# Working a mixture of experts with the weights stationary: Silu straight from PSUM, no turning of the hidden rows, three sets of weight buffers, sixteen groups written out

## What is computed

```python
def _swiglu(x, g, v, o):
    return jax.nn.silu(x @ g) * (x @ v) @ o
scores = jax.nn.softmax(x @ w_router.T, axis=-1)          # 64 experts
topw, topi = jax.lax.top_k(scores, 6)
combine = zeros.at[arange(T)[:, None], topi].add(topw)
routed = sum over 64 experts of combine[:, e] * _swiglu(x, wg[e], wv[e], wo[e])
shared = _swiglu(x, swg, swv, swo)                        # every token
return routed + shared                                     # then layernorm(x + ...)
```

## Time and profile before

| | us |
|---|---|
| median of three runs | 992.77 |
| lowest, highest | 991.32, 993.33 |
| span of the profiled execution, first to last instruction | 985.7 |
| median less span | 7.07 |
| groups of the experts, first weights matmul to last | 521.27 to 698.7 |

### The profile page before, as it was taken

The page is one execution under the profiler, slowest core; times in us unless marked ns, Lnnn a source line. Parts: engine busy times, 40 slices in busy tenths (PEclk is TensorE's granted clock), DMA queues, the critical chain, the costliest instruction groups (busy, mean ns, idle before and its releaser), DMA issues.

```text
span 985.7 us, 15418 instructions
## 1 busy us (share of the span) xinstructions
PE 870.2 (88%) x5267; PEld 568.3 (58%) x5271; DVE 720.6 (73%) x1377; ACT 510.4 (52%) x1022; POOL 407.1 (41%) x338
## 2 busy tenths in 40 slices
PE   7999999999999999988889999999546867899886
PEld 3466666666565666656666777677423654343443
DVE  5667786959696867768774556665467798998797
ACT  3563554545544444445444334455522457898485
POOL 0203448494848577534214333333377312221013
PEclk9999999999999999989999999999866998999998
DMA  5451212112131221100926999999633000000001
GB/s 189 153 196 27 65 49 86 70 65 77 58 102 53 81 75 65 44 1 1 238 94 216 298 311 310 313 312 303 179 96 98 26 1 3 5 8 6 1 6 38
DMA packets 54743, 106.46 MB, mean 108 GB/s; under 512 B 8909, under 2 KB 26645, under 8 KB 54165
## 3 DMA queue, kind: packets, MB, share of 16 engines
q1 hardware_dynamic: 48917, 89.88, 29.6%
q0 software_dynamic: 5760, 15.74, 6.0%
HBM read 88.45 MB, written 17.14 MB: 107 GB/s over the span
## 4 chain that ended last, share of the span: by engine, by line
PE 54%; DVE 19%; DMA 10%; issue 5%; ACT 5%; SPq 3%; POOL 3%; DVEq 0%; ACTq 0%; POOLq 0%
PE ps L777 10%; PE ps L715 6%; DMA w_dn<-in_w_dn 5%; PE ps L873 5%; PE ps L725 4%; DVE row_max L2696 3%; PE ps L948 3%; DMA y_dram<-y_out 3%; PE ps L1280 3%; POOL key_part L1507 2%; DVE state L2119 2%; PE ps L795 2%; PE ps L960 2%; DMA key_part<-y_dram,slot_idx 2%; PE ps L1266 2%
## 5 line engine op out<-in xcount | busy, mean ns | idle before, releaser
L1479 POOL DMA_INDIRECT xg<-x_dram,tok_of x68 | 65.1, 958 | 131.8 <-PE ps L1006 94.2
L777 PE MATMUL ps<-w_vg,xT 128*128 128x512 f32 x256 | 116.8, 597 | 1.2 <-DVE th L2162 1.2
L1429 POOL TENSOR_TENSOR state<-state,rows_bc 128x1024 f32<-128x1024 f32 x22 | 53.8, 2446 | 95.5 <-DVE state L2119 41.9
L715 PE MATMUL ps<-xT,w_qks 128*128 128x512 f32 x192 | 86.5, 596 | 5.2 <-ACT qT L1585 5.2
L948 PE MATMUL ps<-w_gv,xgT 128*128 128x352 f32 (+1 forms) x272 | 87.4, 464 | 2.5 <-DMA w_dn<-in_w_dn 2.4
L2696 DVE TENSOR_REDUCE row_max<-ps 128x4 f32<-128x1024 f32 x64 | 74.3, 1217 | 7.1 <-PE ps L1245 6.3
L2130 DVE TENSOR_TENSOR aT<-ps,tri 128x768 f32<-128x768 f32 x64 | 59.7, 954 | 27.0 <-PE ps L725 26.9
L1585 ACT ACTIVATE probT<-ps 128x512 f32<-128x512 f32 x128 | 69.5, 594 | 10.1 <-PE ps L1266 9.6
L777 PEld LDWEIGHTS ps<-w_vg,xT 128*128 128x128 f32 x256 | 45.8, 190 | 48.8 <-issue 43.1
L960 PE MATMUL ps<-w_dn,hidT 88*128 88x256 f32 (+1 forms) x272 | 70.0, 379 | 0.0
L948 PEld LDWEIGHTS ps<-w_gv,xgT 128*128 128x128 f32 x272 | 48.9, 190 | 27.0 <-issue 5.2
(11 more groups left out here) (327 smaller groups left out, 2066.6 us busy)
## 6 DMA issues: line engine op xcount, KB each, us to landing
w_gv<-in_w_gv SPq DMA_DIRECT2D x68, 352.0 KB, 8.2
rows_bc<-x_dbl_dram SPq DMA_DIRECT2D x32, 512.0 KB, 3.8
w_dn<-in_w_dn SPq DMA_DIRECT2D x68, 192.0 KB, 9.6
y_dram<-y_out SPq DMA_DIRECT2D x68, 128.0 KB, 7.5
y_dram<-blank SPq DMA_DIRECT2D x4, 1408.0 KB, 13.2
w_vg<-in_wvg SPq DMA_DIRECT2D x8, 512.0 KB, 4.9
w_qks<-in_wqks SPq DMA_DIRECT2D x8, 384.0 KB, 3.1
w_o<-in_wo SPq DMA_DIRECT2D x8, 256.0 KB, 2.7
```

Of the source, the lines that this page charges most:

```text
L715: last = mm(bank(PJ + n % 2), w_qks[:, k, part * P:(part + 1) * P], xT[:, k, half * 512:(half + 1) * 512], start=(k == 0), stop=(k == KD - 1))
L777: last = mm(bank(PJ + t % 2), xT[:, k, t * P:(t + 1) * P], w_vg[:, k, :], start=(k == 0), stop=(k == KD - 1))
L1429: G.tensor_tensor(state_of(m), state_of(m), c_row[:, n % 2], ALU.mult).then_inc(read_out, 1)
L1479: G.indirect_dma_start(xg[:, j, :], None, x_dram, bass.IndirectOffsetOnAxis(ap=col, axis=0)).then_inc(gathered[j], 16)
```

## The change

The up projection is turned: the weights are stationary and the activations `xgT` (128 columns) move, so that the hidden values come out with the hidden index on the partitions, as the down projection wants them. The 176 hidden columns are cut in 112 and 64 (`FA`, `FB`). "gate" and "value" of the first 112 go to one PSUM bank for a pair of blocks; "low" has the last 64 of the gate and of the value in one 128-column weight, so that its gate stands on partitions 0 to 63 and its value on 64 to 127. ACT takes Silu directly; DVE multiplies once. `turn_hid`, `hidT_of` and the tanh form are gone, as are the factors 0.5. Down is one matmul of 112 rows for a block and one of 64; the 64-row matmuls of a pair of blocks lie on different rows of the array and write different banks. The work is signalled by pairs of blocks, and the results of a whole group are signalled together: `down_ready` once a group, two copies of 512 columns on DVE, two stores of 256 KB with rows of 2 KB (`y_rows`, `y_pair`), which puts slots in another order, which `slot_idx` takes into account with four more small DVE instructions.

Weights are three DMAs a block: `w_up` 352 KB (rows of 2816 bytes as before), `w_dn` 112 rows of 1 KB, `w_low` 64 rows of 1 KB. `RING` is 3, all twelve blocks are asked for ahead without waits between. For group i SP stores a pair and asks for that pair of group i + 3. Stores 14 and 15 are issued by ACT. The overflow groups all use one set. On PE and SP the sixteen groups are written out. The shared expert is worked the same way, four tiles (512 columns) at once.

```diff
-FH = F // 2
-FP = 96
+HIGH = 64
+FA, FB = F - HIGH, HIGH
+UP = 2 * F
-RING = 2
+RING = 3
+LAST_SET = FIXED % RING
+def y_rows(i, p):
+    rows = y_dram[bass.ds(i * (NJ * P) + p * 2 * P, 2 * P), :]
+    return rows.rearrange("(r two) d -> r (two d)", two=2)
...
-            for dst, src in ((sh_gv, "sh_gv"), (sh_dn, "sh_dn"), (pos, "pos"), (ident_bf, "ident_bf"),
+            for dst, src in ((sh_up, "sh_up"), (sh_dn, "sh_dn"), (sh_low, "sh_low"), (pos, "pos"), (ident_bf, "ident_bf"),
...
             for r in range(RING):
                 for j in range(NJ):
-                    if r:
-                        sp.wait_ge(w_loaded[j], 32 * r)
-                    load_block(r * NJ + j, j, w_gv[:, r * NJ + j], w_dn[:, r * NJ + j])
+                    load_block(r * NJ + j, j, r)
...
-            with sp.Fori(0, FIXED // RING - 1) as d:
-                for r in range(RING):
-                    for j in range(NJ):
-                        store_y(d * RING + r, j)
-                        sp.wait_ge(w_loaded[j], at(d, 32 * RING, 32 * (r + RING)))
-                        sp.sem_inc(load_due, 1)
-                        load_block(d * (RING * NJ) + ((r + RING) * NJ + j), j, w_gv[:, r * NJ + j], w_dn[:, r * NJ + j])
+            for i in range(FIXED - RING):
+                for p in range(2):
+                    store_y(i, p)
+                    sp.wait_ge(w_loaded[i % RING][p], LOADS * (i // RING + 1))
+                    for j in (2 * p, 2 * p + 1):
+                        load_block((i + RING) * NJ + j, j, i % RING)
...
+            def group(i, r, uses):      # PE
...
                 for p in range(2):
+                    pe.wait_ge(xgT_copied, at(i, 2, p + 1))
+                    pe.wait_ge(hid_ready, at(i, 4, HIDDEN - 4 + p + 1))
+                    for o in range(2):
+                        j = 2 * p + o
+                        if o == 0:
+                            pe.wait_ge(w_loaded[r][p], uses * LOADS)
+                        up(ps[0:FA, p, 2 * o * P:(2 * o + 1) * P], w_of(j), "gate", x_of(j))
+                        last = up(ps[0:FA, p, (2 * o + 1) * P:(2 * o + 2) * P], w_of(j), "value", x_of(j))
+                    last.then_inc(up_ready, 1)
+                for p in range(2):
+                    pe.wait_ge(hid_ready, at(i, 4, HIDDEN - 4 + 2 + p + 1))
+                    for o in range(2):
+                        last = up(ps[:, 2 + p, o * P:(o + 1) * P], w_of(2 * p + o), "low", x_of(2 * p + o))
+                    last.then_inc(up_ready, 1)
+                pe.wait_ge(down_copied, at(i, 2, COPIED))
+                for p in range(2):
+                    pe.wait_ge(hid_ready, at(i, 4, HIDDEN + p + 1))
+                    for o in range(2):
+                        mm(ps[:, 4 + o, p * D:(p + 1) * D], hidT_a[:, 2 * p + o, :], w_dn[:, r * NJ + 2 * p + o, :],
+                           start=(p == 0), stop=False, skip_group_check=True)
+                    for o in range(2):
+                        turn_g(i + 1, 2 * p + o)
+                for p in range(2):
+                    pe.wait_ge(hid_ready, at(i, 4, HIDDEN + 2 + p + 1))
+                    for o in range(2):
+                        rows = slice(HIGH * o, HIGH * o + FB)
+                        last = mm(ps[:, 4 + o, p * D:(p + 1) * D], hidT_b[rows, p, :], w_low[rows, r * (NJ // 2) + p, :],
+                                  start=False, stop=True, skip_group_check=True)
+                last.then_inc(down_ready, 1)
...
-            with pe.Fori(0, FIXED // RING) as d:
-                for r in range(RING):
-                    group(d * RING + r, lambda j, k: w_gv[:, r * NJ + j, k, :], lambda j, f: w_dn[0:FH, r * NJ + j, f, :])
+            for i in range(FIXED):
+                group(i, i % RING, i // RING + 1)
...
-            def group(i, side=None):    # ACT
+            def group(i, side=None, stored=None):
                 for p in range(2):
+                    act.wait_ge(up_ready, at(i, 4, HIDDEN + p + 1))
+                    f(silu_a[:, 2 * p:2 * p + 2, :], ps[0:FA, p, :].rearrange("p (e two n) -> p e two n", e=2, two=2)[:, :, 0, :],
+                      ACT.Silu).then_inc(silu_ready, 1)
...
             def group(i, first=False, side=None):       # DVE
-                for j in range(NJ):
-                    hidden(i * NJ + (j + TILES), j, 2 * j + 1)
...
+                dve.wait_ge(down_ready, at(i, 1, 3))
+                if not first:
+                    for p in range(2):
+                        dve.wait_ge(y_stored[p], at(i, 16, 0))
+                for o in range(2):
+                    V.tensor_copy(y_out[:, o::2, :], bank(4 + o).rearrange("p (a d) -> p a d", a=2)).then_inc(down_copied, 1)
+                for p in range(2, 4):
+                    if side:
+                        side(p)
```

More of the change, by code:

```diff
@@ L41 @@
 FIXED = E // NJ
-RING = 2
+RING = 3
+LAST_SET = FIXED % RING
+LAST_USES = len(range(LAST_SET, FIXED, RING))
 FAR = 16384.0
@@ L476, in build @@
         gathered = [sem(f"gathered{j}") for j in range(NJ)]
-        w_loaded = [sem(f"w_loaded{j}") for j in range(NJ)]
-        y_stored = [sem(f"y_stored{j}") for j in range(NJ)]
+        w_loaded = [[sem(f"w_loaded{r}_{p}") for p in range(NJ // 2)] for r in range(RING)]
+        y_stored = [sem(f"y_stored{p}") for p in range(NJ // 2)]
         wkv_loaded = sem("wkv_loaded")
@@ L943, in _, with part_of, up @@
             last.then_inc(route_mm, 1)
-            def gate_up(j, x_of, w):
+            def part_of(w, k, part):
+                first = k * UP + dict(gate=0, value=FA, low=2 * FA)[part]
+                return w[:, first:first + (2 * FB if part == "low" else FA)]
+            def up(out, w, part, x_of):
                 for k in range(KD):
[L948 to L960, removed]
-                last.then_inc(down_ready, 1)
[L963 to L977, removed]
+                    last = mm(out, part_of(w, k, part), x_of(k), start=(k == 0), stop=(k == KD - 1))
+                return last
+            Y_SH = (3, 2)
+            def shared_up(h):
+                def x_of(k):
+                    return xT[:, k, h * 512:(h + 1) * 512]
+                if h:
+                    pe.wait_ge(hid_ready, 2)
+                up(ps[0:FA, 0, :], sh_up, "gate", x_of)
+                up(ps[0:FA, 1, :], sh_up, "value", x_of).then_inc(up_ready, 1)
+                if h:
+                    pe.wait_ge(down_copied, 2)
+                up(bank(2), sh_up, "low", x_of).then_inc(up_ready, 1)
@@ L1005, in turn_g @@
                 for k in range(KD):
-                    last = nc.tensor.transpose(ps[:, 2 * j, k * P:(k + 1) * P], xg[:, j, k * P:(k + 1) * P], ident[:])
+                    last = nc.tensor.transpose(ps[:, 6 + j // 2, (j % 2) * D + k * P:(j % 2) * D + (k + 1) * P],
+                                               xg[:, j, k * P:(k + 1) * P], ident[:])
                 last.then_inc(xg_turned, 1)
[L1009 to L1027, removed]
@@ L1498, in _ @@
                     gather(j, tok_cur[:, j:j + 1])
-            for j in range(NJ):
-                pool.wait_ge(y_stored[j], at(used, 16, 0))
+            for p in range(NJ // 2):
+                pool.wait_ge(y_stored[p], at(used, 16, 0))
             pool.sem_inc(gather_due, 1)
@@ new lines, in _, with xgT_of @@
+            silu_shared(0)
+            scale_probs()
+            keep_shared(0)
+            scale_hot(0)
+            silu_shared(1)
+            for t in range(1, TILES):
+                scale_hot(t)
+            act.wait_ge(angle, 8)
+            f(cos_sin[:], ang[:], ACT.Sin).then_inc(cos_sin_ready, 1)
+            act.wait_ge(route_mm, 3)
+            f(expert_row[:], ps[0:1, Y, 0:P], ACT.Copy).then_inc(route_act, 1)
+            keep_shared(1)
+            def xgT_of(i, p, first=False):
+                act.wait_ge(xg_turned, at(i, NJ, 2 * p + 2))
+                if not first:
+                    act.wait_ge(up_ready, at(i, 4, HIDDEN - 4 + 2 + p + 1))
+                f(xgT[:, 2 * p:2 * p + 2, :].rearrange("p a b -> p (a b)"), bank(6 + p), ACT.Copy).then_inc(xgT_copied, 1)
@@ new lines, in store_late @@
+            def store_late(i):
+                act.wait_ge(down_copied, at(i, 2, COPIED + 2))
+                for p in range(2):
+                    act.dma_start(y_rows(i, p), y_pair(p)).then_inc(y_stored[p], 16)
+            def group(i, side=None, stored=None):
+                for p in range(2):
+                    act.wait_ge(up_ready, at(i, 4, HIDDEN + p + 1))
[3 more added lines that the diff above has]
+                        side(p)
+                for p in range(2):
+                    act.wait_ge(up_ready, at(i, 4, HIDDEN + 2 + p + 1))
+                    f(silu_b[HIGH:P, 2 * p:2 * p + 2, :].rearrange("p a b -> p (a b)"),
+                      ps[0:FB, 2 + p, 0:2 * P], ACT.Silu).then_inc(silu_ready, 1)
+                if stored is not None:
+                    store_late(stored)
+                for p in range(2):
+                    xgT_of(i + 1, p)
```

(11 more changed lines are left out.)

237 lines of the change are left out of this document (127 added, 110 removed).

## The result

| | before | after |
|---|---|---|
| median, 20 runs of each, side by side | 987.92 us | 993.96 us |
| ratio of the two, 95% interval | | 1.0067 [1.0045, 1.009] |
| profiled execution, span | 985.7 us | 993.1 us |
| first gather behind the groups (POOL `key_part`) | 703.93 us | 708.65 us |

The changed kernel is 0.7% **slower**, about 6 us, where 9 us faster was forecast. The forecast set out from 992.77, the median of three runs that lay within 0.2% of each other; twenty runs of the kernel before spread from 979.89 to 993.33, with the median at 987.92. Ratios are therefore the fair measure: forecast 983.8/992.77 = 0.991, measured 1.0067.

A forecast was written before the change was run, and what follows sets the result against it. DMA bandwidth was taken to bound the groups, PE 5% behind. Groups ending 10.3 us earlier, 1.3 given back, made net -9.0: span 976.7 plus 7.07 gave 983.8 us; its own range 977 to 990, with rivals 971 to 992.

The forecast's parts named there:

- rival (c): Groups: stores of y set the pace, landing 8.0 + copies 1.36 + issue 0.7 stretching to 10.44 us; 993 us, chance 10%.
- wrong: List of contrary signs: rate under 300, 9.2 us groups throughout, DMA share under 1 during `y_stored` waits, first `tok_of` after 512.3.
- the sum: Groups: loads from 532.0, 46.0 MB at 309 GB/s until 680.9, then 7.5 us of PE, ending 688.4 instead of 698.7.
- The third set: Weights before the groups: 2.16 MB move into the idle stretch; loads starting later give back 4 of its 7 us.
- The DMA's rate: Groups' full stretch: 309 GB/s, the deciding term; 260 GB/s if reads limit gives 981.6 us, 300 and 320 give 988 and 979.
- PE's group: PE per group: 9.24 us (9.0 to 9.8) instead of 9.96, up 5.4, off the path while DMA needs more.
- the 64-row passes: Down projection: two 256-column pairs side by side on the array take 1.22 us a group, 1.74 if not.
- rival (d): Down projection: 64-row pairs don't run side by side, group 9.76 us, still under 10.39; no time change, no separate chance.
- The start of the groups: After routing: moves by 0 to -1.2 us, taken as -0.6, to 520.7.
- The idle stretch: DMA before the groups, 495 to 512 us, nearly idle (0.06) before: filled to about 500 by the added weight loads.
- From PE's end to the first gather: Behind the groups: 1.3 us more, from DVE copies of 1.36 instead of 0.43 and one more store issue of 0.36.
- Rival (b): Groups: PE is the bound if DMA runs above 350 GB/s; 17 x 9.24 = 157 us, time 973, chance 12%.

The follow-up runs named there:

- the one without its other waits: Changed kernel with second set of `y_out`, empty slots' rows spread, `w_up` loads released after the up passes: two weight sets 1.0033, three 0.9874 to the kernel before.
- The kernel with both causes removed: Changed kernel with a second set of `y_out` and the gathered rows of empty slots spread: 979.08 us, 0.9914 to the kernel before.
- the best version: Changed kernel, three weight sets, with second `y_out`, empty slots' rows spread and `w_up` released when the up passes are done: 974.88 us, 0.9874 to the kernel before.
- the first two runs with two sets: Changed kernel with two weight sets instead of three: 1024.52 us, 1.0362; the same with `w_up` released early, stores ahead of small loads: 992.27 us, 1.0053.
- the kernel before and its variant: The variant is the kernel before with the gathered rows of empty slots spread: 988.7 us, 1.0024 to the kernel before.

## Why the prediction was wrong, point by point

**The failed step is the sentence against rival (c)**: "a store is late only because loads stand ahead of it, and then the DMA is working". It left out the time that SP needs to issue. In the changed order six issues of 0.43 to 0.6 us stand on SP between a group's copies and its second store; while they pass, the DMA is not kept full (0.94 and 0.96 up to 600 us), because SP had waited for those copies before it issued any of that group's loads. The rival's sum had 0.7 us of issue where 3.7 passed, and 8.0 of landing where 5.5 were needed. The two errors nearly cancelled (10.06 against 10.5 measured): that the rival's period came out right was luck, and the argument that set it at 10% was wrong. Its sign stood in the text under "wrong": share under 1 while DVE waits for `y_stored`.

PE ended the groups at 703.15 us, 14.8 later than the 688.4 of the sum. An estimate from the forecast's own terms (first group 9.24, last group 9.24, so 9.95 a step between) divides this: 7.7 us in the fourteen steps that the store loop paces (10.50 each), 4.2 in the step to the overflow group (14.1), 1.3 in the last group at the low clock, and 1.6 before the second group's up pass, as the first group took 11.17 us at a granted clock of 0.83 (521.3 to 531.3 us; 1.00 before).

**The overflow's gathers** were in no term. The sum let PE do 7.5 us behind the last weights; it was gathered rows that came last, 3.1 us of waiting and about 2.3 more at the lower clock. Spreading the rows gave 8 us in the median.

**The third set** was priced as prefetch alone, 7 us with 4 given back. The 4 us were the right observation (results are signalled for a whole group) counted once, for the start. With two sets the late release is a loop that returns every second group; the third set was worth 29 us in this kernel and 16 in the one without its other waits.

**The DMA's rate** was mis-sized the other way: 309 GB/s was taken for a limit. With the wait for the stores gone it was 323, with `w_up` ahead 342. The kernel with both causes removed comes to 0.9914, almost the forecast ratio of 0.991, but by chance in part: in its profile the groups begin at 525.48, 4.8 us later than forecast, and then follow faster, at 9.55 us. The Trainium skill, "DMA: Bandwidth & Descriptors", section "Bandwidth", would price the 64 KB loads at 15 us in all over 309 GB/s, an estimate from its table; the rows speak against it here too, as the same loads queue in the stretch of 342 GB/s.

**What held.** PE's group: 9.14 us against 9.24, up 5.5 against 5.4, the 64-row passes 1.09 to 1.13 against 1.22, so the pairs run side by side and rival (d) falls. The start of the groups, 520.36 against 520.7, in this profile; with a lower clock ahead of them it came up to 5 us later (last section). The idle stretch filled. From PE's end to the first gather 5.5 us instead of 5.2: the 1.3 us more were there, but the last store landed in 2.32 instead of 3.57. Rival (b), PE as the bound, is what the best version comes nearest, though only after three edits more: ratio 0.9874, where the 973 worked out is 0.980 of the base it set out from.

**What stays open.** Why the gathers of the same empty rows are not late in the kernel before, where all land within 7.1 us, nor in the first two runs with two sets, which don't spread them either: there POOL, which waits for the last gather, goes on 7.5 and 6.1 us after issuing it, against 10.0 in the changed kernel. So many entries that name one row are not enough by themselves; what else it takes no run shows. Why the rate rises from 324 to 342 GB/s at the same share of 1.06 when the four large loads of a group are issued together: no run parts the order of the loads from the earlier release.

## What to carry to other kernels

When a store is what frees a buffer, write the whole circle down, from the copy through every instruction that the issuing queue passes to the landing and back, and compare its length with the pace that bytes and matmuls allow; a queue that issues loads between two stores is in that circle. A release that moves from pieces to a whole group lengthens such circles by the issue time of the group, and then a buffer more can be worth much more than the bytes that it prefetches (29 and 16 us here, against some 7). Look at the last, odd group by itself: its gathers may be the slowest of all.

## What was not expected of the hardware

With a second `y_out`, gathers in which the empty entries all name one row took up to 10.4 us to land, and 7.2 when the entries were spread over 128 rows; the step to the overflow group went from 14.7 to 10.7 us. In the kernel before it made no difference (7.0 and 7.1). What makes it so no run shows.

At a share of 1.06 from 560 to 640 us the DMA carried 310 GB/s in the kernel before, and with the loads and stores of the changed kernel 317 with the stores ahead, 323 with a second `y_out` and 342 with the large loads released early: a full share was no proof that the rate was at its limit.

The granted clock of 475.6 to 492.5 us, in code that most of these kernels share, was 1.00 in some profiles and 0.69 to 0.79 in others, and the groups then began at 523.7 to 525.5 instead of 520.4 to 521.7. So the start of a stage is not compared between single profiles here, only paces inside it and medians. Both profiles of the kernel before and its variant had 1.00, of the eleven of the changed kernel and its variants four; whether the change has a part in that, so few profiles don't show.
